# Softmax attention on one core: parts stored one by one, 24-row key loads, and key scores in seven PSUM banks after the last score tile

## The chip, the cores and the metric

The kernel runs on one core of a Trainium2 chip. The metric is the device time of one execution in microseconds (us), given as the median of several runs. Engines are named as in the profile: PE (TensorE), DVE (VectorE), ACT (ScalarE), POOL (GpSimd) and SP (SyncE, which here only issues DMAs); a "q" behind a name is that engine's instruction queue.

## The reference

Six stages follow one another on x of 2 x 1024 tokens and 128 features: a mixture of experts, gated linear attention, the mixture of experts again, a second mixture of experts with eight wider experts, softmax attention, and that second mixture again. Only the softmax attention is touched:

```
q = embedded @ Wq.T + bq        # 2 batches, 16 heads of 8 features, 1024 tokens
k = embedded @ Wk.T + bk
v = embedded @ Wv.T + bv
qk = einsum('bhqd,bhkd->bhqk', q, k) / sqrt(1024)
p = softmax(qk, axis=-1)        # over all 1024 keys
p = p * triu(ones(1024, 1024))  # only then masked: a query keeps keys at or after it
z = einsum('bhqk,bhkd->bhqd', p, v)
out = layernorm(embedded + z) * gamma + beta
```

The softmax maximum and denominator run over all keys; the mask is laid on afterwards.

## The kernel before

**Parts.** Queries and keys are f32 products kept at nearly f32 precision by three bf16 parts each (part 0 the rounded value, parts 1 and 2 the remainders). In `soft()` PE makes eight projections of 128x512 (n = 0..7; batch 0 first, and in each batch queries, w = 0, before keys, w = 1). For each, ACT writes the f32 value QF (L1015) and part 0 (L1018), and DVE makes the remainder RF (L1389), part 1 (L1390) and part 2 (L1391). QF has two slots, so ACT waits for DVE's projection n - 2. SP then stores the three parts of a batch's queries or keys to DRAM with three DMAs of 256 KB (`store_parts`, L499), once all three exist.

**Groups.** The 32 pairs of batch and head are worked in 8 groups of 4 (groups 0 to 3 are batch 0). `load_group` (L503 to L514) brings a group back from DRAM with 12 DMAs: Q3 gets rows (part, feature) three times over, in 3 DMAs of 24 rows (192 KB, L510); K3 gets each key part three times, in 9 DMAs of 8 rows (64 KB, L513). A row is 4 heads of 1024 tokens in bf16, 2 KB each in DRAM. A product over these 72 rows is the sum of all nine pairs of parts. Three groups fit in the ring (Q3R = 3). After group 0 SP issues three DMAs of ones (L521), the parts of batch 1, groups 1 and 2, and then the rows of maxima, in the order of the plan.

**Plan.** `attention_plan` writes out one order for all engines. Its items: A, a score tile of 128 queries x 1024 keys (two PE matmuls, L824) whose row maxima DVE reduces (L1410); S, POOL's split of four tiles' maxima into three bf16 rows (L1536 to L1539); M, their turning on PE (L832), copy on ACT (L1027) and DMA into Q3 (L534); B, key scores of 128 keys x 512 queries with the maximum subtracted (L849), and ACT's exponential (L1041); V, the values and denominators of one step of four B's (L882), which waits for the exponentials of that step and, where the diagonal is in it, for POOL's mask (L1546). Step m runs B(m, 0..3) and then V(m - 1). 22 A's come before the first B(0, 0); the last A stands in step 114 of 0..127. At the end ACT copies z (L1048), PE turns it (L837) and DVE divides (L1424, L1425).

**Banks.** PSUM has eight banks: A and the turning of z use two pairs (0/1 and 2/3) in turn, B and M use banks 4, 5 and 6 in turn (NBB = 3, `ring_number`, `wait_ring` L796), and V gathers in bank 7.

**POOL.** Before the plan POOL adds beta to X (L1506, four of 128x512).

Of the kernel before, what the change touches and what calls it, by code (L numbers as in the profile page):

```python
# [16 lines left out]
P = 128  # L17
B, S = 2, 1024
N = B * S
# [22 lines left out]
Q3R = 3  # L42
# [7 lines left out]
AEND = 12  # L50
NBB = 3
STEPS = [(0, j) for j in range(TB)] + [(1, j) for j in range(TB)]
# [102 lines left out]
def macaron_kernel(nc, x_in, params, f1_pack, f1_b2, out):  # L155
    with ExitStack() as ctx:
# [3 lines left out]
        def sem(name):  # L160
            return ctx.enter_context(nc.semaphore(name))
# [97 lines left out]
        ZT = m(2 * S).rearrange("p (r n) -> p r n", r=2)  # L259
        m.at = max(m.at, SPLIT + 2 * 1024 + 2 * 3 * N // 2)  # L260
        V9 = m(T * H * 9).rearrange("p (t h j) -> p t h j", t=T, h=H)
# [11 lines left out]

        sp0 = ARENA[:, SPLIT:SPLIT + 2 * 1024 + 2 * 3 * N // 2]
        QF = sp0[:, 0:1024].rearrange("p (r n) -> p r n", r=2)
        RF = sp0[:, 1024:2048].rearrange("p (r n) -> p r n", r=2)
        PART = sp0[:, 2048:].bitcast(BF16).rearrange("p (w a n) -> p w a n", w=2, a=3)
        Z = XNT[:, :].rearrange("p (t d) -> p t d", t=T)
# [9 lines left out]
        qd = nc.dram_tensor("q_parts", [H, 3, DH, N], BF16, kind="Internal").ap()  # L288
        kd = nc.dram_tensor("k_parts", [H, 3, DH, N], BF16, kind="Internal").ap()

# [122 lines left out]
        turns = [x for x in plan if x[0] in "AT"]  # L413
        ring = [x for x in plan if x[0] in "BM"]
        ring_number = {x: n for n, x in enumerate(ring)}
        scores = [x for x in turns if x[0] == "A"]
# [40 lines left out]
        def _(sp):  # L457
# [35 lines left out]
            def soft():  # L493

                def store_parts(b, w):
                    sp.wait_ge(parts_done, 2 * (2 * b + w + 1))
                    half = slice(b * S, (b + 1) * S)
                    for a in range(3):
                        sp.dma_start((qd, kd)[w][:, a, :, half], PART[:, w, a, half]).then_inc(parts_stored[b], 16)  # L499

                def load_group(G):

                    sp.wait_ge(parts_stored[G // NG], 6 * 16)  # L503
                    b, ring = G // NG, G % Q3R
                    u, ab = (G % NG) // 2, G % 2
                    heads = slice(8 * u + ab, 8 * u + ab + 7, 2)
                    for c in range(3):
                        row = 3 * DH * c
                        q = qd[heads, :, :, b * S:(b + 1) * S].rearrange("g a d n -> (a d) g n")
                        sp.dma_start(Q3[row:row + 3 * DH, ring, :, :], q).then_inc(ring_loaded[ring], 16)  # L510
                        k = kd[heads, c, :, b * S:(b + 1) * S].rearrange("g d n -> d g n")
                        for a in range(3):
                            sp.dma_start(K3[row + DH * a:row + DH * (a + 1), ring, :, :], k  # L513
                                         ).then_inc(ring_loaded[ring], 16)  # L514

                store_parts(0, 0)
                store_parts(0, 1)
                load_group(0)
# [4 lines left out]
                store_parts(1, 0)  # L523
                store_parts(1, 1)
                for G in range(1, Q3R):
                    load_group(G)
                for x in plan:
                    if x[0] == "M":

                        _, hh, h = x  # L530
                        G, g = divmod(hh, 4)
                        tiles = tiles_of_unit(h)
                        sp.wait_ge(m_copied, maxima_number[hh, h] + 1)
                        sp.dma_start(Q3[MR:MR + 3, G % Q3R, g, tiles[0] * P:(tiles[-1] + 1) * P],  # L534
                                     MT[0:3 * len(tiles), hh % 4, :]).then_inc(m_rows[hh % 4], 16)
                    if x[0] == "V" and x[1] % NS == NS - 1:
                        G = x[1] // NS
                        if G + Q3R < GR:
                            sp.wait_ge(pv_done, NS * (G + 1))
                            load_group(G + Q3R)  # L540

# [14 lines left out]
        def _(pe):  # L556
# [213 lines left out]
            def soft(ln):  # L770
# [25 lines left out]
                def wait_ring(x):  # L796

                    n = ring_number[x]
                    if n < NBB:
                        return  # L800
                    kind, k, i = ring[n - NBB]
                    if kind == "M":
# [6 lines left out]
                for x in plan:  # L809
                    kind, k, i = x  # L810
                    if kind in "AT":
                        n = turn_number[x]
                        slot = 2 * (n % 2)
                        wait_slot(n)
                    elif kind in "BM":
                        bank = 4 + ring_number[x] % NBB
                        wait_ring(x)
                    if kind == "A":
                        G, g = divmod(k, 4)
                        if G not in begun:  # L820
                            begun.add(G)
                            pe.wait_ge(ring_loaded[G % Q3R], 16 * 12 * (G // Q3R + 1))
                        for c in range(2):
# [76 lines left out]
        def _(act):  # L900
# [102 lines left out]
            def soft():  # L1003
# [4 lines left out]
                for n in range(8):  # L1008

                    c, w = 2 * (n // 4) + n % 2, n // 2 % 2  # L1010
                    four = slice(c * 512, (c + 1) * 512)
                    act.wait_ge(proj_done, n + 1)
                    if n >= 2:
                        act.wait_ge(parts_done, n - 1)
                    nc.scalar.activation(QF[:, n % 2, :], PS[:, n % 4, :], ACT.Identity,  # L1015
                                         bias=(BQS[:, :], col("a1_bk"))[w], scale=(S ** -0.5, 1.0)[w]).then_inc(qf_done, 1)
                    act.wait_ge(qf_done, n + 1)
                    nc.scalar.copy(PART[:, w, 0, four], QF[:, n % 2, :]).then_inc(part0_done, 1)  # L1018
                for x in plan:
                    kind, k, i = x  # L1020
                    if kind == "M":
                        act.wait_ge(m_turned, maxima_number[k, i] + 1)
                        before = rows_stored(k, i) - 16
                        if before:
                            act.wait_ge(m_rows[k % 4], before)
                        width = unit_columns(i)[1]
                        nc.scalar.copy(MT[0:width, k % 4, :],  # L1027
                                       PS[0:width, 4 + ring_number[x] % NBB, 0:P // 2].bitcast(BF16)
                                       ).then_inc(m_copied, 1)
                    elif kind == "B":  # L1030
                        n = 4 * k + i
                        act.wait_ge(b_scores, n + 1)
                        if n == 0:

                            for b in range(B):
                                act.wait_ge(parts_stored[b], 6 * 16)
# [4 lines left out]
                        nc.scalar.activation(PT[:, n % NPT, 0:w], PS[:, 4 + ring_number[x] % NBB, 0:w], ACT.Exp  # L1041
                                             ).then_inc(b_exp, 1)
# [20 lines left out]
        def _(dve):  # L1063
# [319 lines left out]
            def soft():  # L1383
                for n in range(8):

                    c, w = 2 * (n // 4) + n % 2, n // 2 % 2
                    four = slice(c * 512, (c + 1) * 512)
                    dve.wait_ge(part0_done, n + 1)
                    link(nc.vector.tensor_tensor(RF[:, n % 2, :], QF[:, n % 2, :], PART[:, w, 0, four], ALU.subtract))  # L1389
                    link(nc.vector.tensor_copy(PART[:, w, 1, four], RF[:, n % 2, :]))  # L1390
                    nc.vector.tensor_tensor(PART[:, w, 2, four], RF[:, n % 2, :], PART[:, w, 1, four], ALU.subtract  # L1391
                                            ).then_inc(parts_done, 1)
                dve.wait_ge(v9_ones, 1)
# [54 lines left out]
        def _(pool):  # L1448
# [37 lines left out]
            def soft():  # L1486
# [131 lines left out]
```

## Time and profile before

| | |
|---|---|
| median of 3 runs | 941.2 us (940.81 to 942.09) |
| profiled execution, own time | 939.37 us |
| its span | 937.6 us |
| PE busy | 661.0 us (70%) |
| DVE busy | 561.3 us (60%) |
| ACT busy | 436.7 us (47%) |
| POOL busy | 318.3 us (34%) |
| mean granted TensorE clock | 0.846 of full |

The profile is one execution. Busy times are sums over the whole span, in which different stages have different limits, so they are read stage by stage: the softmax attention runs from the projections at 372 us to the turning of z at 824 us. "Idle before it" and the releaser say what ended an engine's wait. Granted clock 1.00 is 2.4 GHz and 0.50 is 1.2 GHz.

### The profile page before, as it was taken

The page shows a single profiled execution, that of the slowest core. Times are in us where ns is not written, and L with a number is a line of the kernel's source. Part 1 is how long each engine was busy: PE and PEld are TensorE (multiplying, and loading weights), DVE is VectorE, ACT ScalarE, POOL GpSimd, SP SyncE. Part 2 cuts the span into 40 slices and gives each one's busy share as a digit, 9 for nine tenths or more (in the row PEclk, how much of TensorE's full clock was granted, in tenths as well). Part 3 has the DMA queues.
Part 4 walks back from the last instruction along what each step waited for, and adds up shares of the span by engine and source line. Part 5 has one row for each costly group of instructions (what it writes and reads, how often), then busy time and mean ns, then how long its engine had stood idle before and what let it go on. Part 6 is the DMA issues. An engine that isn't in the chain of part 4 may idle for free.

```text
span 937.6 us, 13816 instructions
## 1 busy us (share of the span) xinstructions
PE 661.0 (70%) x4446; PEld 333.3 (36%) x4446; DVE 561.3 (60%) x1027; ACT 436.7 (47%) x827; POOL 318.3 (34%) x755
## 2 busy tenths in 40 slices
PE   4052767705222983479999999999999999850793
PEld 4041322604222981213333433343333423240793
DVE  5315599631530445677878787879988895051243
ACT  2031501203112651405777677877767678830562
POOL 0516166151623442003141424234342344106242
PEclk9995899656555995756999999999999999975797
DMA  9932500003203001560020201111030000001203
GB/s 233 153 92 47 201 1 0 1 24 93 45 18 93 25 23 45 141 132 17 2 44 10 39 16 22 33 21 33 2 53 2 1 2 2 1 1 42 78 30 98
DMA packets 45927, 44.90 MB, mean 48 GB/s; under 512 B 5904, under 2 KB 36316, under 8 KB 45600
## 3 DMA queue, kind: packets, MB, share of 16 engines
q1 hardware_dynamic: 41168, 35.90, 16.7%
q0 software_dynamic: 4544, 7.60, 3.1%
q8 instruction: 37, 0.61, 0.3%
q10 hardware_dynamic: 144, 0.51, 0.2%
q14 instruction: 34, 0.28, 0.1%
HBM read 27.85 MB, written 17.60 MB: 48 GB/s over the span
## 4 chain that ended last, share of the span: by engine, by line
PE 54%; DVE 18%; issue 8%; POOL 8%; DMA 7%; ACT 2%; SPq 1%; POOLq 0%; DVEq 0%; ACTq 0%
PE PS L882 14%; PE PS L849 11%; PE PS L824 11%; DVE ARENA L1410 5%; PE PS L663 5%; PE PS L674 5%; POOL slots_x L1457 4%; POOL ARENA L1471 2%; PE PS L566 2%; DVE ARENA L1369 2%; DVE XN L1102 2%; DMA ARENA<-slots_x 2%; DVE STATS L1075 1%; DVE PS L1360 1%; DMA ARENA<-k_parts 1%
## 5 line engine op out<-in xcount | busy, mean ns | idle before, releaser
L1410 DVE TENSOR_REDUCE ARENA<-PS 128x1 f32<-128x1024 f32 x256 | 300.9, 1219 | 65.4 <-PE PS L824 64.7
L1041 ACT ACTIVATE ARENA<-PS 128x512 f32<-128x512 f32 x512 | 273.4, 599 | 76.4 <-PE PS L849 71.4
L824 PE MATMUL PS<-ARENA 72*128 72x512 bf16 x512 | 164.6, 405 | 24.0 <-DMA ARENA<-k_parts 17.7
L849 PE MATMUL PS<-ARENA 75*128 75x512 bf16 x512 | 164.9, 384 | 3.4 <-ACT ARENA L1041 3.3
L882 PE MATMUL PS<-ARENA 128*8 128x128 f32 (+8 forms) x1920 | 151.1, 430 | 0.6 <-POOL ARENA L1546 0.6
L1546 POOL TENSOR_SCALAR_AFFINE_SELECT ARENA<-ARENA 128x128 f32<-128x128 f32 x256 | 74.4, 296 | 148.6 <-ACT ARENA L1041 148.3
L615 PE MATMUL PS<-C,ARENA 128*128 128x128 f32 x78 | 17.2, 375 | 116.2 <-DMA ARENA<-slots_x 116.1
L1327 DVE TENSOR_TENSOR ARENA<-PS,ARENA 128x512 f32<-128x512 f32 x46 | 31.8, 692 | 94.5 <-PE PS L663 94.5
L849 PEld LDWEIGHTS PS<-ARENA 75*128 75x128 bf16 x512 | 47.6, 98 | 99.1 <-ACT ARENA L1041 51.2
L824 PEld LDWEIGHTS PS<-ARENA 72*128 72x128 bf16 x512 | 42.5, 99 | 109.1 <-DVE ARENA L1410 39.7
L584 PE MATMUL PS<-C,XN 128*128 128x128 f32 x96 | 24.6, 408 | 80.5 <-DVE XN L1102 79.4
L948 ACT COPY ARENA<-PS 128x512 f32<-128x512 f32 (+1 forms) x20 | 11.5, 573 | 130.3 <-PE PS L615 130.3
L1464 POOL DMA_INDIRECT tokens_y<-ARENA x46 | 44.6, 970 | 74.0 <-DVE ARENA L1336 72.0
L882 PEld LDWEIGHTS PS<-ARENA 128*32 128x32 f32 (+2 forms) x1920 | 43.3, 97 | 73.2 <-issue 41.8
L1536 POOL CAST ARENA<-ARENA 128x4 bf16<-128x4 f32 x64 | 12.6, 196 | 135.5 <-DVE ARENA L1410 135.4
L615 PEld LDWEIGHTS PS<-C,ARENA 128*128 128x128 f32 x78 | 12.7, 193 | 119.2 <-issue 116.3
L663 PE MATMUL PS<-ARENA 128*128 128x128 f32 x368 | 52.8, 290 | 1.1 <-ACT ARENA L971 0.5
L1457 POOL DMA_INDIRECT slots_x<-ARENA,SCATI x32 | 31.4, 981 | 64.6 <-DVE ARENA L1277 56.1
L674 PE MATMUL PS<-ARENA 128*128 x368 | 50.9, 281 | 2.1 <-ACT ARENA L982 2.1
L1483 POOL TENSOR_TENSOR ARENA<-ARENA 128x1024 f32<-128x1024 f32 (+1 forms) x16 | 36.6, 2284 | 40.8 <-DVE ARENA L1369 39.7
L663 PEld LDWEIGHTS PS<-ARENA 128*128 128x128 f32 x368 | 47.3, 202 | 4.7 <-issue 4.6
L1471 POOL DMA_INDIRECT ARENA<-slots_y,GATHI x32 | 32.1, 1002 | 49.3 <-DMA slots_y<-ARENA 40.2
(143 smaller groups left out, 786.5 us busy)
## 6 DMA issues: line engine op xcount, KB each, us to landing
ARENA<-q_parts SPq DMA_DIRECT2D x24, 192.0 KB
ARENA<-k_parts SPq DMA_DIRECT2D x72, 64.0 KB
ARENA<-pack_dram SPq DMA_DIRECT2D x8, 514.0 KB, 6.6
slots_x<-FILL SPq DMA_DIRECT2D x2, 1483.5 KB, 21.7
ARENA<-slots_x SPq DMA_DIRECT2D x10, 258.0 KB, 4.1
ARENA<-slots_x SPq DMA_DIRECT2D x8, 256.0 KB, 3.8
slots_y<-ARENA SPq DMA_DIRECT2D x16, 128.0 KB, 1.8
ARENA<-tokens_y SPq DMA_DIRECT2D x8, 256.0 KB, 3.7
```

The source lines that it names most:

```text
L663: ins = nc.tensor.matmul(PS[:, 4 + i % 2, f * P:(f + 1) * P], W1[:, i % 2, f * P:(f + 1) * P], XST[:, i * P:(i + 1) * P], start=True, stop ...
L674: ins = nc.tensor.matmul(o, HG[:, i % 2, f * P:(f + 1) * P], WT[:, bass.ds(owner[i] * WB + F1 + f * P, P)], start=(f == 0), stop=(f == FB ...
L824: ins = nc.tensor.matmul(PS[:, slot + c, :], Q3[0:KQ, G % Q3R, g, i * P:(i + 1) * P], K3[0:KQ, G % Q3R, g, c * 512:(c + 1) * 512], start=T ...
L849: nc.tensor.matmul(PS[:, bank, 0:w], K3[0:MR + 3, G % Q3R, i, j * P:(j + 1) * P], Q3[0:MR + 3, G % Q3R, i, half * 512:half * 512 + w], sta ...
L882: ins = nc.tensor.matmul(PS[32 * g:32 * g + width, 7, lo:hi], v, probs, start=(what == "denominator" and st in (0, TB)), stop=(j == TB - 1 ...
L1041: nc.scalar.activation(PT[:, n % NPT, 0:w], PS[:, 4 + ring_number[x] % NBB, 0:w], ACT.Exp).then_inc(b_exp, 1)
L1410: nc.vector.tensor_reduce(NM[:, k % 4, i:i + 1], PS[:, slot:slot + 2, :].rearrange("p b n -> p (b n)"), AX.X, ALU.max, negate=True).then_i ...
L1457: pool.indirect_dma_start(sx[k], bass.IndirectOffsetOnAxis(ap=SCATI[:, t:t + 1], axis=0), src[:, t, :], None, bounds_check=slots - 1, oob_ ...
L1464: pool.indirect_dma_start(ty, bass.IndirectOffsetOnAxis(ap=XS[:, i, P:P + 1].bitcast(U32), axis=0), EO[:, i, :], None, bounds_check=N - 1, ...
L1471: pool.indirect_dma_start(YG[:, t, :], None, sy[0:slots, :], bass.IndirectOffsetOnAxis(ap=GATHI[:, t:t + 1], axis=0), bounds_check=slots - ...
L1483: nc.gpsimd.tensor_tensor(QS[:, n % 8, 0:w], QT[:, b * S:b * S + w], ST[:, n % 2, 0:w], ALU.mult).then_inc(qs_done, 1)
L1546: nc.gpsimd.affine_select(out=MD[:, n % NPT, :], in_=PT[:, n % NPT, diag:diag + P], compare_op=ALU.is_ge, fill=0.0, base=0, pattern=[[-1, P]],
```

## The change

Setup:

- SP stores each part as soon as it exists (`store_part`), part 0 first, and key parts 0 and 1 twice: `k_parts` has five places, 0 1 2 0 1. So three consecutive places hold the three parts in turned order, and a group's keys come back in 3 DMAs of 24 rows instead of 9 of 8 rows (`load_k`). Queries (`load_q`) are waited for and issued by themselves, ahead of the keys.
- The ones and all later DMAs wait until group 0 has landed.
- QF has four slots; ACT waits for part 2 of projection n - 4.
- DVE makes the parts of batch 0 only. POOL makes those of batch 1, before it adds beta.

Banks:

- From the last A on, B and M take the least recently used of banks 0 to 6 and wait for that bank's last user, which can be an A (its maximum). Before it, they use 4, 5 and 6 as before.

```
-        parts_done = sem("parts_done")
-        parts_stored = [sem(f"parts_stored{b}") for b in range(B)]
+        part1_done = sem("part1_done")
+        part2_done = sem("part2_done")
+        late_parts = sem("late_parts")
+        parts_stored = [[sem(f"parts_stored{b}{w}") for w in range(2)] for b in range(B)]
...
+        last_tile = max(n for n, x in enumerate(plan) if x[0] == "A")
+        bank_of, bank_user, users = {}, {}, {}
+        for n, x in enumerate(plan):
+            if x[0] in "AT":
+                slot = 2 * (turn_number[x] % 2)
+                users[slot] = users[slot + 1] = n, x
+            elif x[0] in "BM":
+
+                banks = (4, 5, 6) if n < last_tile else (0, 1, 2, 3, 4, 5, 6)
+                bank = min(banks, key=lambda b: users.get(b, (-1, None))[0])
+                bank_of[x], bank_user[x] = bank, users.get(bank, (-1, None))[1]
+                users[bank] = n, x
...
+                def store_part(b, w, a):
                     half = slice(b * S, (b + 1) * S)
+                    for place in ((a,), (a, a + 3))[w and a < 2]:
+                        sp.dma_start((qd, kd)[w][:, place, :, half], PART[:, w, a, half]
+                                     ).then_inc(parts_stored[b][w], 16)
...
+                def load_q(G):
+
+                    b, ring = G // NG, G % Q3R
+                    q = qd[heads_of(G), :, :, b * S:(b + 1) * S].rearrange("g a d n -> (a d) g n")
+                    sp.wait_ge(parts_stored[b][0], 3 * 16)
                     for c in range(3):
+                        sp.dma_start(Q3[3 * DH * c:3 * DH * (c + 1), ring, :, :], q).then_inc(ring_loaded[ring], 16)
+
+                def load_k(G):
+
+                    b, ring = G // NG, G % Q3R
+                    sp.wait_ge(parts_stored[b][1], 5 * 16)
+                    for c in range(3):
+
+                        k = kd[heads_of(G), c:c + 3, :, b * S:(b + 1) * S].rearrange("g a d n -> (a d) g n")
+                        sp.dma_start(K3[3 * DH * c:3 * DH * (c + 1), ring, :, :], k).then_inc(ring_loaded[ring], 16)
+
+                for w in range(2):
+                    sp.wait_ge(part0_done, 2 * (w + 1))
+                    store_part(0, w, 0)
+                    sp.wait_ge(part1_done, 2 * (w + 1))
+                    store_part(0, w, 1)
+                    sp.wait_ge(part2_done, 2 * (w + 1))
+                    store_part(0, w, 2)
+                load_q(0)
+                load_k(0)
+
+                sp.wait_ge(ring_loaded[0], 6 * 16)
...
+                for w in range(2):
+                    sp.wait_ge(late_parts, 2 * (w + 1))
+                    for a in range(3):
+                        store_part(1, w, a)
                 for G in range(1, Q3R):
-                    load_group(G)
+                    load_q(G)
+                    load_k(G)
...
+                for n in range(4, 8):
+
+                    w, four = n // 2 % 2, slice(S + n % 2 * 512, S + (n % 2 + 1) * 512)
+                    pool.wait_ge(part0_done, n + 1)
+                    then(nc.gpsimd.tensor_tensor(RF[:, 2, :], QF[:, n % 4, :], PART[:, w, 0, four], ALU.subtract))
+                    then(nc.gpsimd.tensor_copy(PART[:, w, 1, four], RF[:, 2, :]))
+                    nc.gpsimd.tensor_tensor(PART[:, w, 2, four], RF[:, 2, :], PART[:, w, 1, four], ALU.subtract
+                                            ).then_inc(late_parts, 1)
+                    pool.wait_ge(late_parts, n - 3)
```

## Rows read from the trace of the kernel before

**Rows 1.** The page, part 4: shares of the chain that ended last.
```profile
PE 54%; DVE 18%; issue 8%; POOL 8%; DMA 7%; ACT 2%; SPq 1%; POOLq 0%; DVEq 0%; ACTq 0%
```
**Rows 2.** Waits, 402 to 830 us: total us, times, longest us.
```profile
PE PS L824 <- DMA ARENA<-k_parts: 17.7, 1, 17.7
```
**Rows 3.** The chain in order of time, 358 to 435 us: start, length.
```profile
384.10 3.00 DMA k_parts<-ARENA
...
390.98 11.43 DMA ARENA<-k_parts
...
402.55 1.02 PE PS L824 x2
...
403.60 23.55 DVE ARENA L1410 x20
```
**Rows 4.** Timeline, making the parts: start, length, instruction, count, idle before.
```profile
374.25 0.69 ACT L1015 ACTIVATE ARENA<-PS,ARENA 128x512 f32<-128x512 f32 x1 [2.12 <-PE PS L776]
...
374.97 0.62 ACT L1018 CAST ARENA<-ARENA 128x512 bf16<-128x512 f32 x1
...
375.89 0.69 ACT L1015 ACTIVATE ARENA<-PS,ARENA 128x512 f32<-128x512 f32 x1 [0.31 <-PE PS L776]
...
379.21 0.69 DVE L1389 TENSOR_TENSOR ARENA<-ARENA 128x512 f32<-128x512 f32 x1
...
381.00 0.69 DVE L1389 TENSOR_TENSOR ARENA<-ARENA 128x512 f32<-128x512 f32 x1
...
382.90 1.81 SPq L499 DMA_DIRECT2D k_parts<-ARENA  x3
```
**Rows 5.** The same, SP issuing the first and the last loads of group 0.
```profile
387.11 0.38 SPq L510 DMA_DIRECT2D ARENA<-q_parts  x1
...
390.26 1.02 SPq L513 DMA_DIRECT2D ARENA<-k_parts  x3
```
**Rows 6.** DMA view, 529.9 to 537.9 us in 40 slices: busy tenths, GB/s.
```profile
DMA  0000237568759398688992928667876846446833
GB/s 0 0 0 0 20 82 123 184 246 307 225 102 164 41 102 143 102 92 102 72 72 10 61 20 72 51 82 143 164 133 154 184 82 133 113 82 82 82 41 41
```
**Rows 7.** Windows: length, busy of PE, PEld, DVE, ACT, POOL, clock, DMA share, GB/s.
```profile
413.00:414.00 1.00, 0.93 (x2) 0.13 (x2) 1.00 (x2) 0.00 (x0) 0.70 (x4) 0.50 0.56 129
...
529.50:546.00 16.50, 15.73 (x156) 7.67 (x149) 11.49 (x14) 9.80 (x22) 5.77 (x26) 1.00 0.46 74
```
**Rows 8.** POOL: timeline row of L1506; the page's groups of L1546 and L1483.
```profile
370.31 4.93 POOL L1506 TENSOR_TENSOR X<-X,C 128x512 f32<-128x512 f32 x4 [2.55 <-DVE XN L1102]
...
L1546 POOL TENSOR_SCALAR_AFFINE_SELECT ARENA<-ARENA 128x128 f32<-128x128 f32 x256 | 74.4, 296 | 148.6 <-ACT ARENA L1041 148.3
...
L1483 POOL TENSOR_TENSOR ARENA<-ARENA 128x1024 f32<-128x1024 f32 (+1 forms) x16 | 36.6, 2284 | 40.8 <-DVE ARENA L1369 39.7
```
**Rows 9.** Timeline, the first turned maxima and the first key score.
```profile
411.68 0.27 PE L832 MATMUL PS<-IDB,ARENA 128*12 128x128 bf16 x1
...
428.02 0.63 PE L849 MATMUL PS<-ARENA 75*128 75x512 bf16 x1
```
**Rows 10.** Windows, as Rows 7.
```profile
437.00:438.00 1.00, 1.00 (x12) 0.35 (x5) 0.00 (x0) 0.47 (x2) 0.00 (x0) 0.83 0.00 0
```
**Rows 11.** Timeline, exponentials in threes and fours, values, first and last of the tail.
```profile
431.25 1.57 ACT L1041 ACTIVATE ARENA<-PS 128x512 f32<-128x512 f32 x3 [0.68 <-PE PS L849]
...
790.11 2.07 ACT L1041 ACTIVATE ARENA<-PS 128x512 f32<-128x512 f32 x4 [0.67 <-PE PS L849]
...
797.82 2.06 ACT L1041 ACTIVATE ARENA<-PS 128x512 f32<-128x512 f32 x4 [0.31 <-PE PS L849]
...
798.79 1.04 PE L882 MATMUL PS<-ARENA 128*9 128x512 f32 x8
...
819.97 2.07 ACT L1041 ACTIVATE ARENA<-PS 128x512 f32<-128x512 f32 x4 [0.55 <-PE PS L849]
```
**Rows 12.** The chain, 770 to 835 us: two key scores.
```profile
788.10 0.43 PE PS L849 x2
```

More of the change, by code:

```diff
@@ L504, in load_group, with heads_of @@
+                def heads_of(G):
+                    u, ab = (G % NG) // 2, G % 2
+                    return slice(8 * u + ab, 8 * u + ab + 7, 2)
+                def load_q(G):
                     b, ring = G // NG, G % Q3R
-                    u, ab = (G % NG) // 2, G % 2
-                    heads = slice(8 * u + ab, 8 * u + ab + 7, 2)
+                    q = qd[heads_of(G), :, :, b * S:(b + 1) * S].rearrange("g a d n -> (a d) g n")
+                    sp.wait_ge(parts_stored[b][0], 3 * 16)
@@ L507, in load_group @@
                     for c in range(3):
[L508 to L514, printed above, removed]
@@ L539, in soft @@
                             sp.wait_ge(pv_done, NS * (G + 1))
[L540 removed]
+                            load_q(G + Q3R)
+                            load_k(G + Q3R)
             for kind, ln, k in STAGES:
@@ L796, in wait_ring @@
                 def wait_ring(x):
-                    n = ring_number[x]
-                    if n < NBB:
+                    if bank_user[x] is None:
                         return
-                    kind, k, i = ring[n - NBB]
-                    if kind == "M":
+                    kind, k, i = bank_user[x]
+                    if kind == "A":
+                        pe.wait_ge(a_max, score_number["A", k, i] + 1)
+                    elif kind == "M":
                         pe.wait_ge(m_copied, maxima_number[k, i] + 1)
@@ L815, in soft @@
                     elif kind in "BM":
-                        bank = 4 + ring_number[x] % NBB
+                        bank = bank_of[x]
                         wait_ring(x)
@@ L1012, in soft @@
                     act.wait_ge(proj_done, n + 1)
-                    if n >= 2:
-                        act.wait_ge(parts_done, n - 1)
-                    nc.scalar.activation(QF[:, n % 2, :], PS[:, n % 4, :], ACT.Identity,
+                    if n >= 4:
+                        act.wait_ge(part2_done, n - 3)
+                    nc.scalar.activation(QF[:, n % 4, :], PS[:, n % 4, :], ACT.Identity,
                                          bias=(BQS[:, :], col("a1_bk"))[w], scale=(S ** -0.5, 1.0)[w]).then_inc(qf_done, 1)
                     act.wait_ge(qf_done, n + 1)
-                    nc.scalar.copy(PART[:, w, 0, four], QF[:, n % 2, :]).then_inc(part0_done, 1)
+                    nc.scalar.copy(PART[:, w, 0, four], QF[:, n % 4, :]).then_inc(part0_done, 1)
                 for x in plan:
@@ L1040, in soft @@
                         w = columns(k)[0]
-                        nc.scalar.activation(PT[:, n % NPT, 0:w], PS[:, 4 + ring_number[x] % NBB, 0:w], ACT.Exp
+                        nc.scalar.activation(PT[:, n % NPT, 0:w], PS[:, bank_of[x], 0:w], ACT.Exp
                                              ).then_inc(b_exp, 1)
@@ L1383, in soft @@
             def soft():
-                for n in range(8):
-                    c, w = 2 * (n // 4) + n % 2, n // 2 % 2
-                    four = slice(c * 512, (c + 1) * 512)
+                for n in range(4):
+                    w, four = n // 2, slice(n % 2 * 512, (n % 2 + 1) * 512)
                     dve.wait_ge(part0_done, n + 1)
-                    link(nc.vector.tensor_tensor(RF[:, n % 2, :], QF[:, n % 2, :], PART[:, w, 0, four], ALU.subtract))
-                    link(nc.vector.tensor_copy(PART[:, w, 1, four], RF[:, n % 2, :]))
+                    link(nc.vector.tensor_tensor(RF[:, n % 2, :], QF[:, n, :], PART[:, w, 0, four], ALU.subtract))
+                    nc.vector.tensor_copy(PART[:, w, 1, four], RF[:, n % 2, :]).then_inc(part1_done, 1)
+                    dve.wait_ge(part1_done, n + 1)
                     nc.vector.tensor_tensor(PART[:, w, 2, four], RF[:, n % 2, :], PART[:, w, 1, four], ALU.subtract
-                                            ).then_inc(parts_done, 1)
+                                            ).then_inc(part2_done, 1)
                 dve.wait_ge(v9_ones, 1)
```

33 lines of the change are left out of this document (10 added, 23 removed).

## The prediction

> **What bounds the kernel now.** I read the chain first: PE has 54% of it and DVE 18% [rows 1], so a saving counts only where it moves the chain. Then the waits of the softmax stage, longest single one first: PE stands 17.7 us once, at its first score tile, for the key loads of group 0 [rows 2]. The chain in order of time tells what that wait consists of: key parts stored until 387.10 (384.10 + 3.00), the last load on its way for 11.43 us from 390.98, the first score tile at 402.55, and then 23.55 us of maxima on DVE before key scores begin [rows 3]. From 428 to 790 us PE goes on nearly without a gap; nothing of the change touches that stretch but SP's fewer issues, on which no wait of PE rests. The last stretch with slack is the tail, where no score tile is left and exponentials alternate with waits [rows 11]. So there are two places, one behind the other on the chain, and their gains add.
>
> **Parts of batch 0.** DVE needs 381.00 - 379.21 = 1.79 us a projection and starts the fourth at 381.00, so the last key part is there at 382.8, and the store is issued at 382.90 [rows 4]. DVE's four rounds stay, so this time stays. Gained is only that parts 0 and 1 are issued ahead of it: DVE's part 1 of the fourth projection ends at 382.15, two stores of about 0.6 us each (1.81 us for three [rows 4]) take SP to 383.4 and the last one to 384.0; with 3.0 us to land [rows 3], the keys are in DRAM by about 386.5 (387.0 at worst) instead of 387.10.
>
> **Issue.** Today SP issues 12 loads from 387.11 to 391.3 [rows 5]. Now the three query loads go out at 384.0 to 385.0, while the keys' stores land, and three key loads (0.34 us each) from 386.5 to 387.5. The last issue is 3.8 us earlier.
>
> **Transfer.** This is the term I know least. A group is 576 pieces of 2 KB. A later load of a group, alone on the queues, occupies 0.46 of 16 engines for 16.5 us: 121 engine-us, 0.21 us a piece [rows 7]. But it isn't even: its first query load (24 rows) moves its 192 KB in the six slices from 530.7 on, (20+82+123+184+246+307) x 0.2 us, at a mean share of 0.52, which is 10 engine-us for 96 pieces, 0.10 us each; the slices behind it, mostly 8-row key loads, run at 41 to 164 GB/s with shares as high [rows 6]. And where only key loads are left, the share stands at 0.56 and 129 GB/s [rows 7]: about half of the engines work. So 8 rows use half of the engines, at a poor rate, and 24 rows use more, at a better rate (0.8 in the best slice [rows 6]); I take 12 of 16. Ends: six loads at 0.10 cost 60/12 = 5.0 us, at 0.21 they cost 121/12 = 10.1 us. By the cheap end queries are over by 388.5 and keys land near 391.8; by the dear one, from 386, at 396.3. I take 393.2, nearer the cheap end, since the query load is the same shape. First score tile at 393.3: **9.2 us** earlier (5.9 to 10.8).
>
> The Trainium skill (DMA: Bandwidth & Descriptors, "Why a DMA increments its semaphore by 16 and not by 1") has a load spread over the largest number up to 16 that divides its slowest dimension: 8 engines for 8 rows, 12 for 24. The shares agree [rows 6, 7]. By that rule alone, with one price for every piece, an engine's pieces fall from 60 to 48 and the load from 12.7 to 10.1 us: the dear end.
>
> **Ones and batch 1.** Behind group 0 SP issues ones to about 395.2, eight stores of 0.6 us (today six) to about 400.3, and six loads to about 402.5. At 0.10 to 0.21 us a piece over 12 engines, groups 1 and 2 are in by 412.5 to 422.5. Group 1 isn't needed before 430. But the rows of maxima queue behind these loads, and the first key score waits for them: it is due at 428.02 [rows 9] - 9 = 419. I cost this at nothing; at the dear end it takes back up to 2 us.
>
> **POOL.** ACT loses its waits for DVE and makes a projection each 1.36 us (0.69 + 0.62 and gaps [rows 4]): from 375.89 for n = 1 that is 379.97 for n = 4, part 0 ready at 381.3. POOL then does 12 operations of 128x512. The subtractions are priced by L1506, 4.93/4 = 1.23 us; the cast has no row: below, 0.6 us (L1546 does 128 columns in 0.296), above, 1.23 [rows 8]. Four rounds of 3.3 to 3.9 us with gaps end at 394.6 to 396.9; beta (4.93) ends at 399.5 to 401.9, and the first split (four small operations, 1.05) at 400.6 to 403.0. PE turns its result at 411.68 today [rows 9], which becomes 402.5. So POOL is almost exactly on time; I take off 0.4 us. PE and DVE behind it would stand still for whatever it is late. It is the cover of this edit, and it is thin: every further 0.1 us in an operation is 1.2 us. This also caps the gain: with tiles earlier still, POOL would be last.
>
> The Trainium skill (SBUF — State Buffer, "Who interferes with whom") says that a DVE instruction with two SBUF inputs and a POOL instruction that reads SBUF shut each other out. No row here shows it. POOL's new work meets DVE's last subtractions (381.3 to 382.8), which by that rule would cost it one of them, 0.7 us; DVE's maxima read PSUM.
>
> **Setup in all: 9.2 - 0.4 = 8.8 us.** The 23.55 us of maxima and the half-clock start of the key scores (the granted clock rises at 437 us, 9 us after the first key score [rows 9, 10]) are carried along; a rise 2 us sooner or later is worth 1 us, and lies in the range.
>
> **Tail.** Step 115's exponentials start at 790.11 and step 127's end at 822.04: 13 packs of four, 31.93 us [rows 11]. A pack takes 2.06; three take 1.57 [rows 11], so each further exponential takes 0.49 when its score is ready. Between packs ACT waits 0.31 to 0.67 us, since the fourth score of a step waits for the bank of the first, and the values behind it hold the next step's scores back. With seven banks a whole step of scores stands ready before the values. Then PE needs 1.04 for values and 4 x 0.22 for scores [rows 11, 12], 1.9 us a step against 4 x 0.49 = 1.96 on ACT: ACT is next, with PE just under it (2.1 in the diagonal steps, four at the end, within the slack of one step ahead). 52 x 0.49 = 25.5, + 0.1 for the last to end, 0.4 for two copies of M, 0.5 for the copy of z, 0.1 for the start, is 26.6: **5.3 us** less. Bounds: if the packs keep their 2.07 us, 26.9 + 0.9 and a gain of 4.1; 3.3 if half of the waits stay; 5.8 without the odd terms. What follows (last values, z) stays as it is.
>
> **The sum.** 8.8 + 5.3 = 14.1 us. From the profiled execution's own 939.37 that is 925.3; the median of the runs stands 1.8 us above it, so 941.2 - 14.1 = **927.1**.
>
> **Rivals.** (a) Dear pieces: 24 rows bring only the spread. First tile at 396.5, rows of maxima up to 2 us late: 3.9 to 5.9 + 5.3 gives 930 to 932. For it: one mean price for all pieces; against: the first query load [rows 6]. (b) POOL late but tolerable: 1.6 us an operation, split at 406.6, 4.2 us behind 402.4: 931.3. (c) The seven banks do nothing, as exponentials were bound by values all the same: saving 1 or less, 931.5. Against it: ACT's waits end on key scores, not on banks of probabilities [rows 11]. (d) Slower: POOL's late parts come so late that stores, loads and rows of maxima queue up behind them. At the 2.3 us of L1483 [rows 8] the parts end at 410, SP's stores at 415, its loads at 418, and by 0.21 us a piece groups 1 and 2 are in at 436; the first key score at 437 instead of 428.02, + 9 - 5.3, is 945. It turns slower by over 0.2% once that score comes after 435.2. Against: L1483 has twice the columns. (e) All cheap: 10.8 less POOL's cap, + 5.8: 924.5.
>
> **Chances.** Forecast 0.61 (924.5 to 930), (a) 0.16, (b) 0.08, (c) 0.07, (d) 0.04, (e) 0.04. The range takes in (a), (b) and (c) and about half of (e): 924.4 to 932.5. 0.2% (1.9 us) is what a measurement of this kernel can tell from no change. Slower is (d), 0.04; within 0.2%, a mix of (a) to (c) that eats 12 us, 0.03; faster, 0.93.
>
> **What would show it.** Right: the last key load issued near 387.5 and the first score tile between 392 and 395; an almost full DMA share of 12 engines while group 0 loads; POOL's late parts over by 397 and PE's first turning without a wait; packs of exponentials merging into one row from step 117 on, the end of the last one some 5 us nearer to the last score tile than before. Wrong: PE waiting at L832 for POOL; PE waiting at its first L849 for DMA; ACT still waiting for key scores in the tail; the granted clock rising later than 9 us after the first key score.

## The result and the profile after

| | before | after |
|---|---|---|
| median | 941.2 us (937.82 to 945.66, 9 runs) | 930.47 us (927.37 to 935.67, 9 runs) |
| profiled execution, own time | 939.37 us | 932.09 us |
| its span | 937.6 us | 930.4 us |
| mean granted clock | 0.846 | 0.845 |

The ratio is 0.9893, with a 95% interval of 0.9864 to 0.9921: 10.1 us less (7.4 to 12.8); the medians stand 10.7 us apart. The forecast was 927.1 and 14.1 us less, its range 924.4 to 932.5. The two profiled executions are only 7.3 us apart: that of after lies 1.6 us above its median, that of before 1.8 below. Runs of one kernel differ by 8 us here, and a run below shows a part of the reason.

The chain of the kernel after, 379 to 424 us, in order of time (start, length). It answers to [rows 3].

```profile
379.65 0.44 DVE ARENA L1422
...
381.44 1.28 DVE ARENA L1422
...
383.95 3.27 DMA k_parts<-ARENA
...
387.99 7.12 DMA ARENA<-k_parts
...
395.24 1.03 PE PS L856 x2
...
396.29 23.55 DVE ARENA L1443 x20
...
420.92 2.70 issue
423.62 0.58 PE PS L881
```

Three things to see. The first score tile stands at 395.24 instead of 402.55. One DVE cast takes 1.28 us, where the same cast a round before takes 0.44. And PE stands 2.70 us before the first key score, put down to "issue" because no engine released it: a DMA did (rows_first, below, shows it). So 7.3 us gained at the first tile are 4.4 at the first key score (428.02 [rows 9] to 423.62).

What that DMA waited for shows in the windows of the kernel after (columns as in [rows 7]):

```profile
420.00:421.00 1.00, 0.92 (x2) 0.01 (x1) 1.00 (x2) 0.36 (x1) 0.66 (x4) 0.50 0.79 121
421.00:422.00 1.00, 0.00 (x0) 0.00 (x0) 1.00 (x2) 0.00 (x0) 0.00 (x0) 0.50 0.75 156
422.00:423.00 1.00, 0.00 (x0) 0.00 (x0) 0.18 (x1) 0.00 (x0) 0.00 (x0) 0.50 0.20 38
423.00:424.00 1.00, 0.39 (x2) 0.14 (x3) 0.00 (x0) 0.00 (x0) 0.00 (x0) 0.50 0.01 1
```

The loads of groups 1 and 2 keep the queues at a share of 0.8 until 422.3 us; the rows of maxima, issued behind them, land after that, and the key score starts at 423.62.

The tail, timeline of the kernel after, ACT's exponentials (it answers to [rows 11]):

```profile
787.87 2.07 ACT L1074 ACTIVATE ARENA<-PS 128x512 f32<-128x512 f32 x4 [0.67 <-PE PS L881]
...
790.50 10.13 ACT L1074 ACTIVATE ARENA<-PS 128x512 f32<-128x512 f32 x20
...
800.92 14.01 ACT L1074 ACTIVATE ARENA<-PS 128x512 f32<-128x512 f32 x28
```

The packs are merged into rows of 20 and 28 exponentials with no wait between them. From the start of step 115's pack to the end of the last one: 814.93 - 787.87 = 27.06 us, where it was 31.93. That is 4.9 us less, at 0.50 us an exponential (14.01/28).

The key loads on the two pages, part 6 (count, KB each), before and after:

```profile
ARENA<-k_parts SPq DMA_DIRECT2D x72, 64.0 KB
```
```profile
ARENA<-k_parts SPq DMA_DIRECT2D x24, 192.0 KB
```

Instead of 72 issues of 64 KB there are 24 of 192 KB, as meant.

4.4 and 4.9 would be 9.3, but only 7.1 are left when z is copied (823.45 to 816.34). Between the first key score and step 115's pack the kernel after took 364.25 us and the kernel before 362.09. Nothing was changed there but SP's issues; the granted clock was another. A window of the kernel before, and two of the kernel after:

```profile
685.00:690.00 5.00, 3.52 (x38) 1.30 (x34) 2.65 (x7) 2.32 (x5) 4.12 (x20) 1.00 0.68 98
```
```profile
434.00:435.00 1.00, 1.00 (x4) 0.36 (x3) 0.59 (x1) 0.35 (x2) 0.29 (x1) 0.70 0.01 3
685.00:690.00 5.00, 4.16 (x28) 1.29 (x32) 5.00 (x8) 2.17 (x4) 2.87 (x13) 0.72 0.35 66
```

Before, PE was given full clock 9.3 us after its first key score (at 437.3, [rows 10]); after, 11.0 us (at 434.6), and it lost the clock once more for 3.4 us from 687.2 on. Over the whole stretch that is 9.3 us at half clock before and 14.4 after. The traces of all thirteen kernels here agree that this sets the stretch. It takes 359.1 us with no half clock at all (rows_warm), 360.6 with 3.4 us of it (before_warm, rows_pool_warm), 362.1 and 362.2 with 9.3 and 9.4 (before, rows_first), 362.5 with 10.1 (loads_alone), 364.1 to 364.3 with 14.1 to 14.4 (after, setup_only, keys_8rows, rows_pool) and 364.9 to 365.0 with 14.9 to 15.2 (warm_wait, queries_first, banks_only). So a microsecond at half clock costs about 0.4 us (5.9 over 15.2), and the missing 2.2 us are the clock's.

### The profile page after: what moved, and what is told of

It reads as the page before. It is cut to its first block, busy times and chain, and to the rows that moved or that the text cites. A ratio compares the mean times of both kernels' runs of the same rounds, so it can differ in the third digit from the quotient of the medians.

```text
span 930.4 us, 13775 instructions
## 1 busy us (share of the span) xinstructions
PE 660.7 (71%) x4446; PEld 333.3 (36%) x4446; DVE 555.6 (60%) x1015; ACT 435.1 (47%) x827; POOL 330.6 (36%) x767
## 4 chain that ended last, share of the span: by engine, by line
PE 53%; DVE 18%; issue 9%; POOL 8%; DMA 7%; ACT 3%; SPq 1%; POOLq 0%; ACTq 0%; DVEq 0%
PE PS L914 13%; PE PS L856 11%; PE PS L881 11%; DVE ARENA L1443 5%; PE PS L694 5%; PE PS L705 5%; POOL slots_x L1490 4%; POOL ARENA L1504 2%; PE PS L597 2%; DVE ARENA L1402 2%; DMA ARENA<-slots_x 2%; DVE XN L1135 1%; DVE STATS L1108 1%; DVE PS L1393 1%; ACT ARENA L1074 1%
## 5 line engine op out<-in xcount | busy, mean ns | idle before, releaser
L1490 POOL DMA_INDIRECT slots_x<-XN,SCATI x32 | 31.3, 978 | 50.6 <-DVE SCATI L1330 41.5
```

The source lines that it names most:

```text
L1490: pool.indirect_dma_start(sx[k], bass.IndirectOffsetOnAxis(ap=SCATI[:, t:t + 1], axis=0), src[:, t, :], None, bounds_check=slots - 1, oob_ ...
```

## Experiments

Each was run beside the kernel before, and the ratios are against that (medians of 940.3 to 941.2). "Tile" and "key score" are the first of each in the profiled execution, counted from the first QF (L1015 before), since what lies ahead of it varies by 4 us between executions: from 372.6 to 376.4 us.

| | median | ratio (95%) | tile | key score | PE's wait ahead of it |
|---|---|---|---|---|---|
| before | 941.2 | | 28.3 | 53.8 | none |
| after | 930.5 | 0.9893 (0.9864 to 0.9921) | 21.3 | 49.6 | 2.7 |
| setup_only | 933.0 | 0.9910 (0.9879 to 0.9941) | 21.9 | 52.2 | 4.6 |
| banks_only | 936.2 | 0.9946 (0.9920 to 0.9972) | 27.3 | 52.8 | none |
| rows_first | 928.1 | 0.9872 (0.9843 to 0.9901) | 22.4 | 47.8 | none |
| keys_8rows | 932.2 | 0.9916 (0.9890 to 0.9943) | 22.1 | 49.8 | 2.0 |
| rows_pool | 927.7 | 0.9850 (0.9825 to 0.9874) | 20.9 | 46.4 | none |
| queries_first | 940.2 | 0.9971 (0.9948 to 0.9994) | 26.8 | 52.2 | none |
| loads_alone | 942.4 | 1.0019 (0.9995 to 1.0042) | 27.2 | 56.1 | 3.2 |
| rows_warm | 923.6 | 0.9813 (0.9789 to 0.9838) | 20.9 | 44.8 | none |
| rows_pool_warm | 924.0 | 0.9817 (0.9788 to 0.9845) | 21.4 | 45.2 | none |
| warm_wait | 930.5 | 0.9881 (0.9846 to 0.9916) | 21.2 | 46.1 | none |
| before_warm | 936.4 | 0.9956 (0.9940 to 0.9972) | 27.9 | 51.7 | none |

One execution tells the tile only to about 1 us: the three kernels whose setup is that of before stand at 28.3, 27.9 and 27.3 (before, before_warm, banks_only), the five whose setup is that of after at 21.3, 21.9, 22.4, 20.9 and 21.2 (after, setup_only, rows_first, rows_warm, warm_wait). The means are 27.8 and 21.5, and the gain at the tile is 6.3 us.

### Each part alone

setup_only is the change with the banks left as they were; banks_only is the kernel before with the new banks.

```
-                banks = (4, 5, 6) if n < last_tile else (0, 1, 2, 3, 4, 5, 6)
+                banks = (4, 5, 6)
```

> The setup part of the change alone; scores keep banks 4, 5 and 6 to the end. Theory (the gains of the two places add): first score tile near 395.2 us and first key score near 423.6 us as in the changed kernel, the 13 packs of the tail as long as before (31.9 us); 4.4 us less at the first key score, so 936 to 937.5 where the kernel before has 941.2. Rival (the setup gain is lost again later, so that all of the gain is the tail's): no change, 940 to 941.

> The bank part of the change alone; the setup is that of the kernel before. Theory: first key score at 428.0 us as before, the 13 packs of the tail in 27.1 us instead of 31.9, so 4.9 us less: 936 to 937. Rival (with the banks free, values hold the exponentials back): packs stay at 2.4 us apart, no change.

The setup alone gave 8.5 us (5.5 to 11.4), the banks alone 5.1 (2.6 to 7.5), both 10.1 (7.4 to 12.8). Neither rival stands: each part is worth its own time. The sum of 13.6 lies above the 10.1, but the intervals don't tell them apart. The tail alone is clean: 28 exponentials in 14.01 us as in the kernel after. For the setup I had expected 4.4 us from the profiled pair, which is under the interval: with its 14.4 us at half clock that pair was a poor measure. setup_only's own profiled execution was its slowest (942.23 of 930.56 to 942.23), with 4.6 us in front of its first key score where 2.7 was expected.

### What PE waits for ahead of the key scores: rows_first

Group 2 is loaded once the fourth row of maxima has been issued.

```
-                for G in range(1, Q3R):
-                    load_q(G)
-                    load_k(G)
+                load_q(1)
+                load_k(1)
                 for x in plan:
...
+                        if (hh, h) == (3, 0):
+                            load_q(2)
+                            load_k(2)
```

> The changed kernel, but group 2 is loaded behind the first four rows of maxima instead of ahead of them. Theory (the 2.70 us that PE stands before the first key score are the rows of maxima, queued behind the loads of groups 1 and 2 that end at 422.3 us): the first key score follows the score tile before it without a gap, at about 420.9 us, 2.7 us earlier, and the time is 2.7 us under that of the changed kernel, near 928. Rival (the gap is the ones, or the stores of batch 1): the key score stays at 423.6 and the time at 930.5.

The chain of rows_first:

```profile
396.00 23.55 DVE ARENA L1445 x20
419.55 0.05 issue
419.60 1.03 PE PS L858 x2
420.63 0.43 PE PS L883
```

The key score follows its score tile without a gap, 47.8 us after the first QF where it was 49.6 (its tile came 1.1 us later than in the profile of after), and the median is 928.1. The rows of maxima were the wait, for group 2's load; ones, stores of batch 1 and group 1, still ahead of them, were not. What it is worth in time is less sure: the intervals of 0.9872 and 0.9893 overlap.

### The shape of the key loads: keys_8rows, queries_first, loads_alone

keys_8rows is the change with nine key loads of 8 rows (the two waits that count a group's DMAs are changed to match, not shown):

```
-                        k = kd[heads_of(G), c:c + 3, :, b * S:(b + 1) * S].rearrange("g a d n -> (a d) g n")
-                        sp.dma_start(K3[3 * DH * c:3 * DH * (c + 1), ring, :, :], k).then_inc(ring_loaded[ring], 16)
+                        for a in range(3):
+                            row = 3 * DH * c + DH * a
+                            k = kd[heads_of(G), c + a, :, b * S:(b + 1) * S].rearrange("g d n -> d g n")
+                            sp.dma_start(K3[row:row + DH, ring, :, :], k).then_inc(ring_loaded[ring], 16)
```

> The changed kernel with each group's keys loaded in nine DMAs of 8 rows as before; all else as changed (double stores too). Theory (the shape matters, 0.17 us a piece over 12 engines against 0.21 and more over 8): group 0's last key load is issued 2 us later and lands 3 to 5 us later, the first score tile near 399 us; groups 1 and 2 end near 430 us and hold the rows of maxima back, so the first key score comes near 431 us, 7 us later than in the changed kernel: 937 to 938. Rival (the earlier issue was what mattered, not the shape): first score tile at 396 to 397, time 932.

I expected 3 to 5 us at the tile and was wrong: 22.1 lies among the five kernels with 24 rows (20.9 to 22.4, mean 21.5). The rival stands. From the first key load's issue to the tile it is 8.9 us with 8 rows (386.92 to 395.81), and 7.5 to 9.0 with 24 in those five. DMA views of one later load of a group, alone on the queues, in 40 slices of 0.4 us from its issue on; the kernel before, keys_8rows and the kernel after:

```profile
DMA  0065757888745876556545554555647510000000
GB/s 0 0 61 174 256 133 118 148 102 77 46 31 67 159 102 138 113 113 72 56 82 61 77 77 72 133 113 92 72 51 128 61 19 1 0 0 0 8 0 0
```
```profile
DMA  0065878778745556456455564420001000000000
GB/s 0 0 77 205 292 149 128 123 149 179 174 97 128 102 92 108 87 87 118 82 97 108 82 118 72 77 36 0 0 0 41 0 0 0 0 0 0 8 0 0
```
```profile
DMA  0055798797788788777830000000000100000000
GB/s 0 0 77 159 297 195 128 143 149 128 195 195 143 154 159 159 138 138 169 189 47 5 0 0 0 0 0 0 0 0 0 41 0 0 0 0 0 8 0 0
```

These loads end after 13.0, 10.8 and 8.6 us. One load is a thin sample: over the five later loads of each kernel it is 12.3 to 13.5, 10.7 to 12.2 and 8.0 to 8.9. So on quiet queues the 24 rows do bring about 3 us, and some 1.4 come with 8-row loads too; on later loads keys_8rows differs from the kernel before in that the three query loads go first (and in `k_parts`' five places). In the last slices of keys_8rows, where only keys are left, a piece isn't dear at all: share 0.4 to 0.6 at 72 to 118 GB/s, against 0.7 to 0.8 at 138 to 189 in the kernel after. More engines, as much data for each.

queries_first gives the kernel before that order and nothing else:

```
                     for c in range(3):
                         row = 3 * DH * c
                         q = qd[heads, :, :, b * S:(b + 1) * S].rearrange("g a d n -> (a d) g n")
                         sp.dma_start(Q3[row:row + 3 * DH, ring, :, :], q).then_inc(ring_loaded[ring], 16)
+                    for c in range(3):
+                        row = 3 * DH * c
                         k = kd[heads, c, :, b * S:(b + 1) * S].rearrange("g d n -> d g n")
```

> The kernel before, but each group's three query loads are issued ahead of its nine key loads; same shapes, same waits. Theory (a good part of what the faster load brought was the order, not the 24 rows: keys_8rows loads a later group in 10.8 us, the kernel before in 13.0, the changed one in 8.6): a later group in about 10.8 us, and group 0's first score tile 1 to 2 us earlier after the last store than before: 939 to 940. Rival (keys_8rows gained by something else, its separate waits or the missing traffic of batch 1): 13.0 us and 402.5, no change.

A later load took 10.6 to 12.4 us, and over five of them the engines spent 91 to 105 engine-us each where the kernel before spent 112 to 121. The order matters, and not by any wait: the same 12 DMAs cost the engines less when like ones stand together. What it brings group 0 is not shown: the tile stands at 26.8, 1.5 us under before but only 0.5 under banks_only. The time fell by 2.7 us by its ratio (0.6 to 4.9), yet the medians are 0.3 apart.

loads_alone holds back the ones and all behind them, in the kernel before, by one line, `sp.wait_ge(ring_loaded[0], 12 * 16)`.

> The kernel before, but the ones and all DMAs behind them are issued only once group 0 has landed, as in the changed kernel. Theory (ones and batch 1's stores slow the load of group 0): from the first load's issue to the first score tile 13.5 us instead of 15.4. The traffic behind comes 9 us later, so the rows of maxima queue behind groups 1 and 2 and the first key score comes later than in the kernel before: 2 us gained at the first tile, some 5 lost at the first key score, time 943 to 945. Rival (the queues serve DMAs strictly in their order, so what is behind costs nothing): 15.4 us and still the loss behind it.

From the first load's issue to the tile it took 14.3 us (386.75 to 401.04) against 15.4. But banks_only, which has the whole queue behind group 0, took 14.4, and before_warm 14.9: that the traffic behind slows group 0 is not shown, and neither rival is ruled out. The loss behind is there, with a wait of 3.2 us ahead of the key score, and no gain in the time.

### DVE and POOL side by side: rows_pool

`pool.wait_ge(part2_done, 4)` ahead of POOL's parts, on top of rows_first.

> As rows_first, and POOL also waits for DVE's fourth part 2 before it begins on batch 1. In the changed kernel DVE's cast of the last key part beside POOL's first subtraction took 1.27 us instead of 0.43, and the store of key part 1 went out that much later. Theory (the two shut each other out): the cast takes 0.43 us again, keys are stored and loaded 0.8 us earlier, POOL ends 1.5 us later and is still in time for the first split (it had 1.9 us to spare): first score tile 0.8 us earlier, time 0.8 under rows_first. Rival (POOL's time is the tighter): PE waits for POOL at its first turning and the gain is gone or negative. Third view (it was chance): the cast stays at 1.3.

Timeline of the kernel after:

```profile
380.94 1.48 POOL L1539 TENSOR_TENSOR ARENA<-ARENA 128x512 f32<-128x512 f32 x1 [13.44 <-ACT ARENA L1050]
...
381.44 1.27 DVE L1422 CAST ARENA<-ARENA 128x512 bf16<-128x512 f32 x1
...
384.82 1.15 POOL L1539 TENSOR_TENSOR ARENA<-ARENA 128x512 f32<-128x512 f32 x1
```

and of rows_pool:

```profile
382.41 0.43 DVE L1424 CAST ARENA<-ARENA 128x512 bf16<-128x512 f32 x1
...
383.65 1.16 POOL L1542 TENSOR_TENSOR ARENA<-ARENA 128x512 f32<-128x512 f32 x1 [15.18 <-DVE ARENA L1426]
```

The two slowed each other: DVE's cast from 0.43 to 1.27 us, POOL's subtraction from 1.15 to 1.48. It wasn't chance: the cast takes 1.27 us in all six kernels without POOL's wait and 0.43 in the two with it. The last key part's store was issued 9.1 us after the first QF instead of 10.0. But it landed no sooner: after 13.0 us here and 13.4 in rows_pool_warm, against 13.0 to 13.4 in the kernels without the wait, so the key loads gained nothing, and 927.7 can't be told from 928.1. The cause of the long cast is shown; it costs nothing that can be seen at the tile. Why the earlier store takes longer to land (3.88 us against 3.27) was not tried; it shares the queues with the other stores and the query loads.

### The clock: rows_warm, warm_wait, before_warm, rows_pool_warm

PE gets work whose results are overwritten: here ten f32 matmuls while it waits for group 0, and one half as wide behind each score tile up to the first key score (rows_warm; rows_pool_warm has POOL's wait too).

```
+                def warm(count, width):
+                    for _ in range(count):
+                        nc.tensor.matmul(PS[:, 7, 0:width], ident, XNT[:, 0:width], start=True, stop=True)
+                warm(10, 512)
...
+                    if kind == "A" and 0 < at < first_b:
+                        warm(1, 256)
```

> As rows_first, and PE does ten f32 matmuls of 512 columns while it waits for group 0 and one of 256 columns behind each score tile up to the first key score; their results go to bank 7 and are overwritten. Theory (the key scores begin at half clock only because PE had stood idle, and this costs half of the 9 to 15 us until the clock rises): the granted clock stays at 1.00 from 372 us on, score tiles keep DVE's 1.18 us, and step 5 is reached 4.5 to 5.5 us earlier: near 923. Rival (PE's share in the score tiles is too low to hold the clock, or the clock falls with whatever is idle before): clock 0.50 at the first key score all the same, fillers of 0.86 us beside tiles of 0.86 us slow PE to 1.7 us a tile, and the time is 5 to 10 us above rows_first.

> rows_warm without the fillers between the score tiles: only the ten in the wait for group 0. PE is then busy 0.43 us of each 1.18 at full clock. Theory (the clock follows what PE does, so the thin stretch of score tiles lets it fall): full clock at the first tile, down to 0.50 within the 25 us of tiles, key scores begin at half clock and the time is that of rows_first, 928. Rival (the ten fillers suffice): clock 1.00 at the first key score, 923.6.

> The kernel before with fillers alone: 17 f32 matmuls of 512 columns in PE's wait for group 0 and one of 256 behind each of the first score tiles. Theory (the late rise of the clock is a cost of its own, 9 to 15 us at half clock in the kernel before as well, and most of the spread between its runs): 4.5 to 7.5 us under the kernel before, 933 to 936, with its runs closer together. Rival (the fillers helped rows_warm by something else): no change at 940.5.

> rows_first with both: POOL waits for DVE's last part, and the fillers keep PE's clock. Theory (the 0.85 us on DVE's cast and the half-clock start are separate): 0.8 us under rows_warm, near 922.8, and no half-clock stretch before 800 us. Rival (with keys and tiles earlier, POOL is the last at the first turning): PE waits for POOL's first split, time as rows_warm or above.

Windows of rows_warm and of warm_wait (the granted clock stands ahead of the last two numbers):

```profile
396.00:419.50 23.50, 22.43 (x90) 10.84 (x89) 23.12 (x21) 2.30 (x5) 7.33 (x22) 1.00 0.55 144
419.50:440.00 20.50, 19.57 (x161) 7.27 (x162) 17.20 (x16) 15.19 (x30) 7.29 (x31) 1.00 0.26 59
```
```profile
396.00:400.00 4.00, 2.30 (x9) 0.54 (x8) 3.17 (x3) 0.00 (x0) 4.00 (x4) 1.00 0.25 50
400.00:404.00 4.00, 2.66 (x7) 0.49 (x8) 4.00 (x5) 0.00 (x0) 0.94 (x5) 0.72 0.98 322
408.00:420.00 12.00, 11.13 (x24) 1.56 (x23) 12.00 (x11) 1.33 (x4) 1.55 (x8) 0.50 0.35 73
```

With fillers between the tiles the clock stayed at 1.00 and PE was busy 22.4 of 23.5 us; without them it stood at 1.00 for the first 5.6 us of tiles, with PE busy 2.30 of 4.00, and then fell to 0.50, and stayed there until 435.9. rows_warm stands at 923.6, 4.5 us under rows_first. Its trace says where: 1.6 us between the first tile and the first key score (25.5 to 23.9), and 3.1 between that and step 115's pack (362.2 to 359.1). warm_wait gains nothing: 930.5. Fillers alone took 4.1 us (2.6 to 5.6) off the kernel before (17 of them in its longer wait), just under the 4.5 to 7.5 expected, and its twelve runs lie within 3.7 us where the seventeen of the kernel before beside them lie within 7.6. So the late clock is a cost of its own, in both kernels, and in the kernel before about half of the spread between runs. (The five runs of rows_warm lie within 2.0 us, but so do the four of rows_first, within 1.8.) rows_pool_warm isn't faster than rows_warm (its profile lost the clock once near 680 us); rows_warm is the best version run, 0.9813 (0.9789 to 0.9838).

## Why the prediction was right, and where it was off

The time lay inside the range, and the sign and both places of the gain were right. The gain was taken too large by 4 us (14.1 against 10.1). The result isn't in the band of the forecast itself (924.5 to 930) but in that of rival (a), 930 to 932, which the range took in. Two of the signs of being wrong came true: PE waited for a DMA at its first key score, and the clock rose later than 9 us after it (11.0). By its steps, in the profiled executions:

- **Parts.** "DVE's four rounds stay, so this time stays" failed by 0.85 us: POOL's first subtraction held up DVE's last cast (rows_pool). I had looked at this very meeting and charged it to POOL (0.7 us), not to DVE, which is the one on the chain. It cost both: POOL's first three operations took 3.65 us where the next three took 2.91. The rule that I quoted from the Trainium skill (SBUF — State Buffer, "Who interferes with whom") speaks of DVE instructions with two SBUF inputs, and the subtractions agree with it; the one held up on DVE's side is a cast with one input, which the same section lists among those that can take the shared ports. It also says that issue order decides who blocks, and the cast began at 381.44, behind POOL's 380.94. But the whole step gained nothing anyway. I had the keys in DRAM 0.6 us earlier; counted from the first QF they landed after 12.9 us in before and after 13.0 to 13.4 in every kernel with the new setup, those with POOL's wait too.
- **Issue.** Keys in DRAM at 387.22 instead of 386.5; the last load issued at 387.9 instead of 387.5. Counted from the first QF, the last issue is 2.7 us earlier than before, not 3.8.
- **Transfer.** The size was near (a load alone takes 8.0 to 8.9 us, my ends were 5.0 and 10.1), the reason mostly wrong, and with it the near hit is partly luck. The 24 rows shorten a load on quiet queues by 3 us, but they didn't make group 0 come early: with 8 rows the tile stands 0.6 us behind the mean of the others, inside their spread. The rest of the 6.3 us is left to the order of the loads, the empty queue behind them, and the earlier issue (the queries' by 2.2 us, the last key load's by 2.7); how it divides among these no run here shows. The price of 0.10 us a piece was wrong too: it was read from the first query load, and the first slices of the 24-row load above run as fast (297 GB/s) while the whole of it doesn't. Whole loads with 24 rows cost 86 to 98 engine-us in the kernel after, 0.15 to 0.17 a piece. And I left out how long a DMA takes to be reported: the queues are empty at 393.8 and the last load counts as landed at 395.1. That is most of 393.3 against 395.24. The rule of the Trainium skill on the number of engines (DMA: Bandwidth & Descriptors, "Why a DMA increments its semaphore by 16 and not by 1") comes near the shares (0.8 for 24 rows, where 12 of 16 is 0.75; 0.5 for 8), and yet its 12.7 to 10.1 us is not what happened to group 0.
- **Behind group 0.** "I cost this at nothing" was the largest miss: 2.7 us (rows_first). The mechanism stood in the text, and its figures too: groups 1 and 2 in between 412.5 and 422.5, the key score due at 419. I took the cheap end for both; they were in at 422.3. At 0.18 us a piece (0.8 of 16 engines for 16.3 us, 1152 pieces) my own working gives 402.5 + 17.3 = 419.8, already past 419. And SP was late: it issued the last of the stores at 402.8 and the last of the loads at 409.7, not at 400.3 and 402.5. The kernel before had the warning. It loads the same two groups, and its queues are free of them only at 426 us, 2 us ahead of its key score at 428.02:

```profile
425.00:426.00 1.00, 1.00 (x3) 0.09 (x1) 1.00 (x2) 0.00 (x0) 0.00 (x0) 0.50 0.25 48
426.00:427.00 1.00, 1.00 (x3) 0.13 (x2) 1.00 (x1) 0.79 (x2) 0.00 (x0) 0.50 0.00 0
```

  A key score 9 us earlier needed those loads earlier by about 7.
- **POOL.** Right: casts of 0.61 us, subtractions of 1.15, parts over at 394.1; PE's first turning waited for nothing, so the 0.4 us taken off weren't needed. The cover held with 1.9 us to spare.
- **Tail.** 4.9 us instead of 5.3; a ready exponential takes 0.50 us, not 0.49, and the two copies of M took 0.56 us instead of 0.4.
- **Carried along.** The half-clock start was taken as fixed, with 1 us for its drift. It drifts more than that: from 9 to 15 us over the kernels here. In the profiled pair this and the second loss of the clock hid 2.2 us of the gain.

Added up: 14.1 less 2.2 at the tile (9.2 against 7.0 from the first QF), 2.7 behind it and 0.4 in the tail, and 0.4 back for POOL, is 9.2; the clock takes 2.2 of it in the profiled pair, which leaves 7.0, where 7.1 were seen (6.8 from the first QF). The runs as a whole, with 10.1 (7.4 to 12.8), agree with the 9.2.

Rival (a) was nearest: it had the tile at 396.5 and the rows of maxima up to 2 us late, by 0.21 us a piece; measured are 395.2, 2.7 and 0.15 to 0.18. (b), (c), (d) and (e) didn't happen.

## What to carry to other kernels

- When transfers are moved behind a barrier to speed up the first, ask what small DMA of the critical path is issued behind them: here 3 KB of maxima waited for 2.3 MB nobody needed yet, and issuing them ahead of half of it took a wait of 2.7 us away.
- Before pricing a transfer by its shape, run it with the shape alone changed. Here the old shape kept all but 0.6 of the 6.3 us at the first tile, though the new one is 3 us faster on quiet queues.
- PE, waiting for a DMA, paid twice here, for the wait and for the clock it gave up; fillers that are overwritten were worth 4 to 5 us, nearly as much as the banks, but only where they went on until the key scores began.

## What the runs showed of the hardware

- The loads of one group (busy share x 16 engines x time, five later groups each) cost 109 to 125 engine-us when 24-row and 8-row ones alternate, 91 to 110 when the three 24-row ones go first, and 83 to 100 when all have 24 rows. Why the order costs engine time wasn't tried further and stays open.
- PE's granted clock rose from 0.50 between 9.3 and 15.2 us after the first key score (9.3 and 9.4 in before and rows_first, 10.1 to 11.0 in loads_alone, setup_only, keys_8rows, rows_pool and after, 15 in banks_only, queries_first and warm_wait); in before and after PE was busy without a gap all that time. What decides it within a kernel stays open. It is what made the stretch of key scores 359.1 to 365.0 us long in the thirteen traces, at about 0.4 us for each microsecond at half clock.
- In six of the thirteen traces the clock fell to 0.50 for 3.4 us once more, between 678 and 694 us (after, setup_only, keys_8rows, rows_pool, rows_pool_warm, before_warm).
- DVE's maxima were a little faster at PE's full clock: a tile each 1.13 us in rows_warm, rows_pool_warm and before_warm, 1.17 in warm_wait and 1.18 in the others.
